# Gathers over more tiles, ELU's operations after the third block sum, ScalarE's block copies first at step 5

## The chip, the cores and the metric

The kernel runs on one core of a Trainium2 chip. The metric is the time of one execution on the device in microseconds, the median of several runs. A profiled execution gives the times of single instructions.

## The reference, cut to what matters

2048 samples, 10 time steps, tables for region and point of interest, a convolution over three steps with ELU, then two LSTM layers of 256 units over 8 steps, and three linear layers with no nonlinearity between them.

```
rp = concatenate([region_tbl[region_idx], poi_tbl[poi_idx]], -1)
nv = concatenate([rp @ W_rp + b_rp, coords @ W_co + b_co], -1)
conv = elu(conv1d(nv, conv_w) + conv_b)
emb = tanh(concatenate([car_tbl[car_idx], week_tbl[week_idx], time_tbl[time_idx]], -1))
x = concatenate([conv, broadcast(emb)], -1)
h = lstm_layer(x, Wih0, Whh0, bih0, bhh0)
h = lstm_layer(h, Wih1, Whh1, bih1, bhh1)
return ((h[:, -1] @ W1 + b1) @ W2 + b2) @ W3 + b3
# lstm step: i, f, g, o = split(x @ Wih.T + h @ Whh.T + bias)
#            c = sigmoid(f) * c + sigmoid(i) * tanh(g);  h = sigmoid(o) * tanh(c)
```

## The kernel before

The samples are worked on in four batches of 512 columns, numbered 0 to 3 (in `stages`, `n`). Every engine runs its own list of instructions, written out by hand; all of them walk through the same list of stages, and semaphores tie them together. There is no scheduler: the order in the code is the order on the engine.

A **cell** is one step of one layer. Layer 0's cell of step t ("lower") and layer 1's cell of step t-1 ("upper") alternate. A cell has eight tiles: two halves j of the state for each of the four gates, 128 x 512 each. After a tile TensorE raises `gate_acc[0]` or `gate_acc[1]`, which VectorE, ScalarE and the gathers wait for. All products are of fp16 high and low parts, three for each fp32 product.

In steps 1 to 5 of batches 1 to 3 (steps 4 and 5 in batch 0) the upper cell is a **fast** one (`fast_cell` in TensorE's part): fourteen block products of 128 x 256 in the manner of Strassen, twelve matmuls each, and not 192 matmuls of 512 columns. It uses PSUM banks A1, A2 (in `aux`) and B1, B2, E1, E2 (in `acc`). The first two products fill A1 and A2. ScalarE copies A1 to B1 and A2 to B2 (`upper_acts`, L1006); the third product adds to B1 and so waits for the first copy, the fourth for the second. Later ScalarE copies E1, A1, E2 and A2 into `gates1` (L1013 to L1022). VectorE adds the second form to them in `part_sums` (L1622), four sums in a cell; the twelfth product reuses A1 and waits for the second of these sums.

VectorE's part of the stages is `lower` (eight `add_embeddings`, L1379, one for each tile of the lower cell, between the operations of the upper cell before it) and `upper`. In both, `both_ig`, `both_fc`, `both_c`, `both_h` and `both_lo` are the LSTM's elementwise operations over 128 x 1024, and `t_forms`, `t_low` make sums of h's blocks for the next fast cell.

Three things for the following batch lie between these:

- **ELU** of the second half of the features (`elu_piece`, nine pieces numbered 0 to 8, 1 to 4 being a reciprocal over 128 columns each, 5 and 6 a product and a sum, 7 and 8 the high and low part of the result). VectorE does pieces 0 to 3 in the lower cell of step 2 and the others in `upper` of step 1 (`low.makes_x`), in batches 1 to 3. SyncE then loads the result into `x_in`; step 4 is the first to use it.
- **The turn**: before step 5's upper cell TensorE transposes the gathered features and embeddings of the next batch (`turn`, c = 0, and `turn_emb`). ScalarE copies the features out of PSUM (`put_turned`) and takes two tanh of the embeddings (`emb_tanhs`); VectorE makes the low part (`split_emb`). That is in batches 0 to 2. The second half of the features is turned in the next batch, after its first upper cell.
- **Gathers** (GpSimd, `pool` in the code, POOL in the rows): per batch 8 of the embeddings and 48 of region and point of interest for the first six time steps, then 32 for the last four. Each is an indirect DMA of 128 rows. `pace` names cells as (layer, step); before a gather POOL waits until the tile that the generator `tiles` gives it has been made. Step 8 and 9 mean steps 0 and 1 of the next batch.

Of the kernel before, what the change touches and what calls it, by code (L numbers as in the profile page):

```python
# [47 lines left out]
ADDS7 = 4  # L48
# [11 lines left out]
class Cell:  # L60
# [3 lines left out]
    def __init__(self, layer, t, counts, bank0, before, slots=None, first=False, last=False, batch=None,  # L64
# [8 lines left out]
        self.forms_of = None  # L73
        self.opens7 = False
        self.early = False
        self.makes_x = False
# [78 lines left out]
def stages(eng, nbatch, steps):  # L155
# [10 lines left out]
    def body(n, following, opened=None):  # L166
# [50 lines left out]
        if following:  # L217
            yield "turn", n + 1, 0
            yield "turn_emb", n + 1
        end = fast(last_t - 2)  # L220
        yield "upper", end, low[1]
        low = lower(last_t, end)
# [37 lines left out]
def build(nc, d):  # L260
# [20 lines left out]
    GR = NCOL // P  # L281
# [14 lines left out]
    with ExitStack() as ctx:  # L296
# [365 lines left out]
        def _(pool):  # L662
# [66 lines left out]
            for n in range(NB):  # L729
# [64 lines left out]
                else:  # L794
# [7 lines left out]
                    if n == 1:  # L802
                        pool.wait_ge(idx_ready, 3)
                    begun = list(pace(n, [(0, 3), (1, 2), (0, 4), (1, 3), (0, 5), (1, 4)]))
                    rows = GR * (2 + 2 * WIN)
# [4 lines left out]
                    copy_emb()  # L810
                    tiles = pace(n, [(1, 5), (0, 7), (1, 6), (0, 8)])
                    gather_steps(WIN, T, True, rows_in[1])

        @block.scalar
        def _(act):
# [185 lines left out]
            def upper_acts(s, low):  # L1001
                steps, sums = s.fast * STEPS7, s.fast * ADDS7
                act.wait_ge(h_done[1], ahead + s.half)
                for bank, source, step in ((B1, A1, 1), (B2, A2, 2)):
                    act.wait_ge(part_acc, steps + step)
                    nc.scalar.copy(bank, source).then_inc(part_copy, 1)  # L1006
                for bank, pair, step in ((B1, (GATE_I, GATE_G), 3), (B2, (GATE_F, GATE_O), 4)):
                    act.wait_ge(part_acc, steps + step)
                    for a, g in enumerate(pair):
                        quarter(s, 0, g, LEFT, half_bank(bank, a))  # L1010
                tanh_both(low)
                act.wait_ge(part_acc, steps + 5)
# [86 lines left out]
            for stage in stages(act, NB, STEPS):  # L1099
                kind = stage[0]  # L1100
                if kind == "turn":
                    n, c = stage[1:]
                    put_turned(feat_t[:, c, :], aux[0:KF, c, :], turned[c], n + 1, turned_put[c])
                elif kind == "turn_emb":
                    emb_tanhs(stage[1], aux[:, 2, :])
                elif kind == "emb_gates":
                    put_emb_gates(*stage[1:])
                elif kind == "conv":
                    elu_parts(chunk_of(*stage[1:]), slice(0, NCOL))
                elif kind == "lower":  # L1110
                    lower_acts(*stage[1:])
                elif kind == "upper":
                    upper_acts(*stage[1:])
                elif kind == "rest":
                    tanh_both(stage[1])
                    put_h_hi(stage[1])
                elif kind == "cell":
                    final_acts(stage[1]) if stage[1].final else cell_acts(stage[1])

        @block.vector  # L1120
        def _(dve):
# [463 lines left out]
            def lower(s, tail, plain_tail):  # L1585
# [17 lines left out]
                else:  # L1603
# [6 lines left out]
                    for k, place in enumerate(places[4:]):  # L1610
                        add_embeddings(s, *place)
                        if s.makes_x:
                            elu_piece(chunk_of(s.batch, 1), s.batch, k)
# [10 lines left out]
            def upper(s, low):  # L1624
# [3 lines left out]

                x_piece(4)
                both_ig(low)  # L1630
                both_fc(low)
                both_c(low)
                x_piece(5)
                x_piece(6)
                both_h(low)
                if low.forms is not None:
                    t_forms(low)
                both_lo(low)
                x_piece(7)
                part_sums(s, 0)  # L1640
                if low.forms is not None:
                    t_low(low)
                x_piece(8)
                for k in range(1, ADDS7):
                    part_sums(s, k)
                both_ig(s)

# [98 lines left out]
            for stage in stages(dve, NB, STEPS):  # L1746
                kind = stage[0]
                if kind == "turn_emb":
                    split_emb(stage[1])
                elif kind == "conv":  # L1750
                    n, c = stage[1:]
# [559 lines left out]
```

## Time and profile before

| what | us |
|---|---|
| median of 3 runs | 1069.15 (1068.37 to 2749.66) |
| the profiled execution | 1068.24 |
| its span, first to last instruction | 1066.4 |
| TensorE busy in it | 1027.5 |
| VectorE, ScalarE, GpSimd busy | 810.0, 668.1, 351.0 |

The median is that of the runs shown, the longest of which is disturbed. In the rows, PE is TensorE (PEld its weight loads), DVE VectorE, ACT ScalarE, POOL GpSimd. Batch 1's steps lie from about 337 us, batch 2's from 587, batch 3's from 836; one batch takes some 249 us.

### The profile page before, as it was taken

How to read it: one execution, taken by the hardware profiler on the slowest of the kernel's cores; microseconds unless marked ns; L12 is line 12 of the kernel's file. 1: busy time of each engine (PE TensorE's matmuls, PEld its weight loads, DVE VectorE, ACT ScalarE, POOL GpSimd, SP SyncE). 2: the span in 40 equal slices, each digit the busy share in tenths (PEclk: the TensorE clock that was granted, in tenths of full speed). 3: DMA queues.
4: the chain of work that ended last, by engine and by line, in shares of the span. 5: the costliest groups of instructions: out<-in, count | busy, mean ns of one | idle time of the engine just before them, and what ended most of it. 6: DMA issues, size and time to landing. Idle time of an engine off the chain costs nothing.

```text
span 1066.4 us, 15685 instructions
## 1 busy us (share of the span) xinstructions
PE 1027.5 (96%) x6129; PEld 627.9 (59%) x6129; DVE 810.0 (76%) x1135; ACT 668.1 (63%) x1029; POOL 351.0 (33%) x353
## 2 busy tenths in 40 slices
PE   8699999999999999999999999999999999999997
PEld 6444444477445666676545567766644577666645
DVE  5489889976768878677787886777686887878654
ACT  2466444577565767777664676767755577777743
POOL 7660066645430046553540025663631000000000
PEclk9799999999999999999999999999999999999999
DMA  9310100000111010000010110000010100000001
GB/s 258 80 18 14 30 3 2 3 2 2 14 21 40 2 33 2 3 2 2 2 32 1 40 32 3 3 3 2 3 31 2 40 22 10 1 1 2 1 1 40
DMA packets 32092, 21.43 MB, mean 20 GB/s; under 512 B 19629, under 2 KB 25865, under 8 KB 32019
## 3 DMA queue, kind: packets, MB, share of 16 engines
q1 hardware_dynamic: 21223, 19.25, 6.3%
q0 software_dynamic: 9984, 1.12, 2.7%
q8 instruction: 48, 0.79, 0.3%
q14 instruction: 25, 0.20, 0.1%
q10 hardware_dynamic: 812, 0.07, 0.1%
HBM read 9.92 MB, written 4.19 MB: 13 GB/s over the span
## 4 chain that ended last, share of the span: by engine, by line
PE 80%; DVE 11%; issue 4%; ACT 4%; another core or an unknown queue 0%; DVEq 0%; POOL 0%; ACTq 0%; POOLq 0%
PE acc L1967 29%; PE acc L2001 13%; PE aux L2001 13%; PE acc L1958 12%; PE acc L1952 4%; DVE gates L1379 2%; PE aux L2282 2%; PE acc L1779 2%; ACT gates L938 1%; DVE h_part L1581 1%; DVE t_part L1546 1%; DVE h_full L1574 1%; PE acc L2107 1%; PE acc L2116 1%; PE aux L1867 1%
## 5 line engine op out<-in xcount | busy, mean ns | idle before, releaser
L1967 PE MATMUL acc<-h_part,wh 128*128 128x512 f16 x1824 | 445.9, 380 | 0.0
L1967 PEld LDWEIGHTS acc<-h_part,wh 128*128 128x128 f16 x1824 | 160.4, 98 | 217.6 <-issue 53.5
L740 POOL DMA_INDIRECT feat<-in_L_rec_region_tbl,region_idx x160 | 173.6, 1085 | 148.8 <-PE aux L2001 45.8
L1379 DVE TENSOR_TENSOR gates<-acc,emb_gates 128x512 f32<-128x512 f32 x239 | 157.1, 682 | 22.8 <-PE acc L1967 16.1
L938 ACT ACTIVATE gates<-gates,gate_bias,unscale 128x512 f32<-128x512 f32 x168 | 128.3, 806 | 65.0 <-DVE gates L1379 62.8
L740 POOL DMA_INDIRECT feat<-in_L_rec_poi_tbl,poi_idx x120 | 132.4, 1103 | 93.5 <-PE acc L1967 33.9
L1958 PE MATMUL acc<-h_part,wh 128*128 128x512 f16 x624 | 148.6, 379 | 0.3
L1952 PE MATMUL acc<-x_in,wx 96*128 96x512 f32 x239 | 132.8, 562 | 0.8 <-DVE gates L1379 0.8
L923 ACT ACTIVATE gates<-acc,gate_bias,unscale 128x512 f32<-128x512 f32 x110 | 81.8, 780 | 77.1 <-PE acc L1967 54.0
L1958 PEld LDWEIGHTS acc<-h_part,wh 128*128 128x128 f16 x624 | 59.8, 98 | 75.5 <-issue 4.4
L2001 PE MATMUL aux<-t_part,w_form 128*128 128x256 f16 x816 | 94.8, 273 | 0.0
L966 ACT ACTIVATE gates<-gates,gate_bias,unscale 128x256 f32<-128x256 f32 x136 | 75.2, 593 | 25.1 <-DVE gates L1622 23.7
L1574 DVE TENSOR_TENSOR h_full<-gates 128x1024 f32<-128x1024 f32 x38 | 46.6, 1227 | 53.9 <-ACT gates L945 50.0
L2001 PEld LDWEIGHTS aux<-t_part,w_form 128*128 128x128 f16 x816 | 79.8, 98 | 9.5 <-ACT gates L1022 0.3
L923 ACT ACTIVATE gates<-gates,gate_bias,unscale 128x512 f32<-128x512 f32 x74 | 57.3, 810 | 33.8 <-DVE gates L1379 29.9
L2001 PE MATMUL acc<-h_part,wh 128*128 128x256 f16 x408 | 49.4, 278 | 13.3 <-ACT acc L1006 9.5
L1952 PEld LDWEIGHTS acc<-x_in,wx 96*128 96x128 f32 x239 | 45.2, 190 | 27.7 <-issue 2.2
L1581 DVE TENSOR_TENSOR h_part<-h_full,h_part 128x1024 f16<-128x1024 f32 x38 | 46.4, 1222 | 15.2 <-ACT h_part L951 15.2
L932 ACT ACTIVATE gates<-cell_c 128x512 f32<-128x512 f32 x50 | 31.4, 627 | 40.9 <-DVE cell_c L1408 24.0
L945 ACT ACTIVATE gates<-cell_c 128x1024 f32<-128x1024 f32 x38 | 40.1, 1056 | 21.0 <-DVE cell_c L1567 20.0
L2001 PEld LDWEIGHTS acc<-h_part,wh 128*128 128x128 f16 x408 | 38.9, 99 | 23.8 <-ACT acc L1006 13.8
L2001 PE MATMUL aux<-t_part,wh 128*128 128x256 f16 x408 | 50.1, 273 | 2.8 <-DVE gates L1622 2.8
(239 smaller groups left out, 1451.7 us busy)
## 6 DMA issues: line engine op xcount, KB each, us to landing
out<-y SPq DMA_DIRECT2D x16, 256.0 KB, 2.1
x_in<-conv_hi SPq DMA_DIRECT2D x56, 64.0 KB
feat<-in_L_rec_region_tbl,region_idx POOLq DMA_INDIRECT x160
w<-in_L_rec_W SPq DMA_DIRECT2D x4, 512.0 KB, 5.2
w_nat<-in_L_rec_Whh SPq DMA_DIRECT2D x2, 1024.0 KB, 8.3
w<-in_L_rec_W SPq DMA_DIRECT2D x1, 2048.0 KB
feat<-in_L_rec_poi_tbl,poi_idx POOLq DMA_INDIRECT x120
x_in<-conv_lo SPq DMA_DIRECT2D x28, 64.0 KB
```

Of the source, the lines that this page charges most:

```text
L740: pool.indirect_dma_start(out, None, tables[k], bass.IndirectOffsetOnAxis(ap=rows, axis=0)).then_inc(landed, DMA)
L923: nc.scalar.activation(gates[layer][:, j, g, :], source, ACT.Tanh if g == GATE_G else ACT.Sigmoid, bias=gate_bias[:, layer, m:m + 1], scal ...
L938: nc.scalar.activation(gates[0][:, j, g, :], gates[0][:, j, g, :], ACT.Tanh if g == GATE_G else ACT.Sigmoid, bias=gate_bias[:, 0, m:m + 1] ...
L945: nc.scalar.activation(gates[layer][:, :, GATE_I, :], cell_c[layer][:, :, :], ACT.Tanh).then_inc(tanh_c_done[layer], HK)
L966: op = nc.scalar.activation(gates[1][:, j, g, cols], source, ACT.Tanh if g == GATE_G else ACT.Sigmoid, bias=gate_bias[:, 1, m:m + 1], scal ...
L1379: nc.vector.tensor_tensor(gates[0][:, j, g, :], source, emb_gates[:, g * HK + j, :], ALU.add).then_inc(gate_sum, 1)
L1574: nc.vector.tensor_tensor(h_full[:, :, :], gates_of(s, GATE_O), gates_of(s, GATE_I), ALU.mult).then_inc(h_full_done[layer], HK)
L1581: nc.vector.tensor_tensor(h_part[layer][:, s.write_slot, LO, :, :], h_full[:, :, :], h_part[layer][:, s.write_slot, HI, :, :], ALU.subtrac ...
L1952: mm = nc.tensor.matmul(bank, wx[:, rows], x_in[:, s.t, :], start=True, stop=s.first)
L1958: mm = nc.tensor.matmul(bank, wh[:, 1, a, c, rows], h_part[0][:, s.write_slot, b, c, :], start=(c == 0 and a == b == HI), stop=(s.first an ...
L1967: mm = nc.tensor.matmul(bank, wh[:, own_w, a, c, rows], h_part[layer][:, s.read_slot, b, c, :], start=False, stop=(c == HK - 1 and a == LO))
L2001: mm = nc.tensor.matmul(bank[:, cols], weights(left, layer, w, g), moving(right, layer, x), start=(opens and a == layer == 0 and w == x == ...
```

## The change

Three edits, and no matmul moves.

First, the gathers' generator. The first set of 56 was spread over the 48 tiles of (0,3), (1,2), (0,4), (1,3), (0,5), (1,4); now over 60, from (1,1) to the fourth tile of (0,6). The second set of 32 took one tile after the other of (1,5), (0,7), (1,6), (0,8), 30 tiles; now it is spread over 44, to the sixth tile of (0,9).

Second, on VectorE ELU's pieces 5 and 6 stand after the third block sum and not before `both_h`, piece 7 after the fourth sum, piece 8 after `both_ig`, piece 4 after `both_c`.

Third, at step 5's upper cell ScalarE makes the copies A1 to B1 and A2 to B2 first, then the feature copy, four gate activations, and then the two tanh of the embeddings. VectorE's `split_emb` stands behind `both_c`. The cell knows by `feeds` for which batch.

```diff
         end = fast(last_t - 2)
+        end.feeds = n + 1 if following else None
         yield "upper", end, low[1]
...
-                    begun = list(pace(n, [(0, 3), (1, 2), (0, 4), (1, 3), (0, 5), (1, 4)]))
+                    begun = list(pace(n, [(1, 1), (0, 3), (1, 2), (0, 4), (1, 3), (0, 5), (1, 4), (0, 6)]))[:-4]
                     rows = GR * (2 + 2 * WIN)
                     tiles = (begun[i * len(begun) // rows] for i in range(rows))
...
-                    tiles = pace(n, [(1, 5), (0, 7), (1, 6), (0, 8)])
+                    begun = list(pace(n, [(1, 5), (0, 7), (1, 6), (0, 8), (1, 7), (0, 9)]))[:-2]
+                    rows = GR * 2 * (T - WIN)
+                    tiles = (begun[i * len(begun) // rows] for i in range(rows))
...
                     act.wait_ge(part_acc, steps + step)
                     nc.scalar.copy(bank, source).then_inc(part_copy, 1)
+                if s.feeds is not None:
+                    put_turned(feat_t[:, 0, :], aux[0:KF, 0, :], turned[0], s.feeds + 1, turned_put[0])
                 for bank, pair, step in ((B1, (GATE_I, GATE_G), 3), (B2, (GATE_F, GATE_O), 4)):
...
+                if s.feeds is not None:
+                    emb_tanhs(s.feeds, aux[:, 2, :])
                 tanh_both(low)
...
-                        if s.makes_x:
+                        if s.makes_x and k < 3:
                             elu_piece(chunk_of(s.batch, 1), s.batch, k)
...
-                x_piece(4)
+                x_piece(3)
                 both_ig(low)
                 both_fc(low)
                 both_c(low)
-                x_piece(5)
-                x_piece(6)
+                if s.feeds is not None:
+                    split_emb(s.feeds)
+                x_piece(4)
...
-                x_piece(7)
                 part_sums(s, 0)
                 if low.forms is not None:
                     t_low(low)
+                part_sums(s, 1)
+                part_sums(s, 2)
+                x_piece(5)
+                x_piece(6)
+                part_sums(s, 3)
+                x_piece(7)
+                both_ig(s)
                 x_piece(8)
-                for k in range(1, ADDS7):
-                    part_sums(s, k)
-                both_ig(s)
```

How the order on the engines changes, at the two places that the prediction speaks of. On ScalarE, step 5's upper cell, before: the `feat_t` row is the feature copy, `emb_tanh` and `emb_in` the two tanh, `acc<-aux` the copies of A1 and A2.

```order
L938 ACTIVATE gates<-gates,gate_bias,unscale 128x512 x5
L879 COPY feat_t<-aux 84x512
L900 ACTIVATE emb_tanh<-aux 128x512
L901 ACTIVATE emb_in<-aux 128x512
L1006 COPY acc<-aux 128x512 x2
L966 ACTIVATE gates<-acc,gate_bias,unscale 128x256 x4
L945 ACTIVATE gates<-cell_c 128x2x512
L1013 COPY gates<-acc 128x2x256
```

And after:

```order
L942 ACTIVATE gates<-gates,gate_bias,unscale 128x512 x5
L1010 COPY acc<-aux 128x512 x2
L883 COPY feat_t<-aux 84x512
L970 ACTIVATE gates<-acc,gate_bias,unscale 128x256 x4
L904 ACTIVATE emb_tanh<-aux 128x512
L905 ACTIVATE emb_in<-aux 128x512
L949 ACTIVATE gates<-cell_c 128x2x512
L1021 COPY gates<-acc 128x2x256
```

The two block copies went to the front, and the two tanh now stand directly before the cell state's tanh (`gates<-cell_c`).

On VectorE, step 1's upper cell, from `both_h` on, before. `elu_part`, `conv_hi` and `conv_lo` are ELU's pieces 5 to 8, `gates<-acc,gates` and `gates<-aux,gates` the block sums.

```order
L1352 SCALAR_TENSOR_TENSOR elu_part<-elu_part 128x512
L1357 TENSOR_TENSOR elu_part<-elu_part 128x512
L1574 TENSOR_TENSOR h_full<-gates 128x1024
L1533 TENSOR_TENSOR t_full<-h_full 128x512
L1536 TENSOR_TENSOR t_full<-h_full,t_full 128x256
L1539 TENSOR_TENSOR t_full<-h_full,t_full 128x256
L1581 TENSOR_TENSOR h_part<-h_full,h_part 128x1024
L1361 CAST conv_hi<-elu_part 128x512
L1622 TENSOR_TENSOR gates<-acc,gates 128x2x256
L1546 TENSOR_TENSOR t_part<-t_full,t_part 128x1024
L1364 TENSOR_TENSOR conv_lo<-elu_part,conv_hi 128x512
L1622 TENSOR_TENSOR gates<-aux,gates 128x2x256 x2
```

And after:

```order
L1588 TENSOR_TENSOR h_part<-h_full,h_part 128x1024
L1629 TENSOR_TENSOR gates<-acc,gates 128x2x256
L1553 TENSOR_TENSOR t_part<-t_full,t_part 128x1024
L1629 TENSOR_TENSOR gates<-aux,gates 128x2x256 x2
L1359 SCALAR_TENSOR_TENSOR elu_part<-elu_part 128x512
L1364 TENSOR_TENSOR elu_part<-elu_part 128x512
L1629 TENSOR_TENSOR gates<-acc,gates 128x2x256
L1368 CAST conv_hi<-elu_part 128x512
L1561 TENSOR_TENSOR ig<-gates 128x1024
L1371 TENSOR_TENSOR conv_lo<-elu_part,conv_hi 128x512
L1567 TENSOR_TENSOR cell_c<-gates,cell_c 128x1024
```

The last four pieces went behind the second and third sum, two of them behind the fourth sum too. POOL's list keeps its order; only the tile that each gather waits for is another.

## Rows read from the trace of the kernel before

**Rows 1.** The page: busy times (us, share, instructions), and the chain that ended last.

```profile
PE 1027.5 (96%) x6129; PEld 627.9 (59%) x6129; DVE 810.0 (76%) x1135; ACT 668.1 (63%) x1029; POOL 351.0 (33%) x353
...
PE 80%; DVE 11%; issue 4%; ACT 4%; another core or an unknown queue 0%; DVEq 0%; POOL 0%; ACTq 0%; POOLq 0%
```

**Rows 2.** Windows: steps 2 to 4 of batches 1, 2, 3; length, then busy times.

```profile
391.00:490.20 99.20, 93.41 (x674) 65.44 (x673) 73.58 (x92) 70.53 (x108) 54.57 (x52) 1.00 0.04 3
640.50:739.50 99.00, 94.34 (x674) 66.35 (x673) 73.92 (x92) 70.57 (x108) 55.08 (x51) 0.98 0.05 3
889.80:982.50 92.70, 92.55 (x673) 65.78 (x672) 73.59 (x92) 70.64 (x108) 0.00 (x0) 1.00 0.00 1
```

The columns are window, length, busy time and count of PE, PEld, DVE, ACT and POOL, then the granted clock of TensorE, DMA share and GB/s.

**Rows 3.** Windows, TensorE alone: single cells. Length, busy, granted clock, DMA share, GB/s.

```profile
411.40:423.80 12.40, 12.40 (x59) 1.00 0.04 2
423.80:444.70 20.90, 18.65 (x170) 1.00 0.04 3
...
491.00:510.10 19.10, 18.48 (x171) 1.00 0.03 2
640.50:662.90 22.40, 19.84 (x169) 0.92 0.05 4
...
675.30:694.10 18.80, 18.66 (x170) 1.00 0.05 3
...
889.80:908.30 18.50, 18.45 (x169) 1.00 0.00 1
```

The first is a lower cell, the others are fast upper cells.

**Rows 4.** Timeline of batch 1, start of step 3's upper cell: start, length, instruction, idle before.

```profile
423.85 2.78 PE L2001 MATMUL aux<-h_part,wh 128*128 128x256 f16 x24
...
424.58 0.95 POOL L740 DMA_INDIRECT feat<-in_L_rec_poi_tbl,poi_idx  x1 [0.30 <-issue]
...
425.83 1.25 POOL L740 DMA_INDIRECT feat<-in_L_rec_region_tbl,region_idx  x1 [0.30 <-issue]
...
428.26 0.57 ACT L1006 COPY acc<-aux 128x512 f32<-128x512 f32 x1 [2.06 <-remote]
428.88 2.29 PE L2001 MATMUL acc<-h_part,wh 128*128 128x256 f16 x18 [2.25 <-issue]
...
430.03 0.94 POOL L740 DMA_INDIRECT feat<-in_L_rec_region_tbl,region_idx  x1 [1.70 <-PE acc L2001]
```

**Rows 5.** Timeline of batch 1, step 1's upper cell; last row batch 3's lower cell.

```profile
362.00 2.79 PE L2001 MATMUL acc<-h_part,wh 128*128 128x256 f16 x24 [0.77 <-ACT acc L1006]
...
371.19 0.42 DVE L1361 CAST conv_hi<-elu_part 128x512 fp32r<-128x512 f32 x1
...
373.38 0.68 DVE L1364 TENSOR_TENSOR conv_lo<-elu_part,conv_hi 128x512 fp32r<-128x512 f32 x1
373.98 1.28 DVE L1622 TENSOR_TENSOR gates<-aux,gates 128x512 f32<-128x512 f32 x2
...
374.72 1.48 PE L2001 MATMUL aux<-t_part,wh 128*128 128x256 f16 x12 [0.76 <-DVE gates L1622]
...
377.55 0.69 DVE L1622 TENSOR_TENSOR gates<-acc,gates 128x512 f32<-128x512 f32 x1 [2.29 <-PE acc L2001]
...
882.34 0.69 DVE L1379 TENSOR_TENSOR gates<-acc,emb_gates 128x512 f32<-128x512 f32 x1 [0.40 <-PE acc L1967]
```

**Rows 6.** Timeline of batch 1, the turn and step 5's upper cell.

```profile
492.14 0.97 POOL L740 DMA_INDIRECT feat<-in_L_rec_region_tbl,region_idx  x1 [11.58 <-PE aux L2001]
492.37 0.56 ACT L879 COPY feat_t<-aux 84x512 f32<-84x512 f32 x1
...
493.80 1.06 ACT L1006 COPY acc<-aux 128x512 f32<-128x512 f32 x2
494.01 1.40 DVE L1372 TENSOR_TENSOR emb_in<-emb_tanh,emb_in 32x512 fp32r<-32x512 f32 x2 [2.61 <-ACT emb_in L901]
494.44 2.79 PE L2001 MATMUL acc<-h_part,wh 128*128 128x256 f16 x24 [0.62 <-ACT acc L1006]
```

**Rows 7.** Waits over the whole span: us in total, times, longest us.

```profile
POOL feat L740 <- DMA feat<-in_L_rec_region_tbl,region_idx: 8.5, 5, 2.4
```

More of the change, by code:

```diff
@@ L74, in __init__ @@
         self.opens7 = False
+        self.feeds = None
         self.early = False
@@ L1102, in _ @@
                     n, c = stage[1:]
-                    put_turned(feat_t[:, c, :], aux[0:KF, c, :], turned[c], n + 1, turned_put[c])
-                elif kind == "turn_emb":
-                    emb_tanhs(stage[1], aux[:, 2, :])
+                    if c == 1:
+                        put_turned(feat_t[:, 1, :], aux[0:KF, 1, :], turned[1], n + 1, turned_put[1])
                 elif kind == "emb_gates":
@@ L1747, in _ @@
                 kind = stage[0]
-                if kind == "turn_emb":
-                    split_emb(stage[1])
-                elif kind == "conv":
+                if kind == "conv":
                     n, c = stage[1:]
```

## The prediction

> **What bounds the kernel now.** Read the page first: TensorE is busy 1027.5 of 1066.4 us, and the chain that ended last is 80% its own [rows 1]. So the kernel is bound by TensorE, and a change that touches no matmul can only give back TensorE's idle time, 38.9 us in all, a good part of it in the opening and at the last head, which the change leaves alone. Two per cent, which is about what a measurement of this kernel can tell from no change, would be 21.4 us.
>
> Next the same work in different batches. From the start of step 2's upper cell to the turn before step 5's (three upper and three lower cells), batches 1, 2 and 3 run the same 670-odd matmuls. They take 99.20, 99.00 and 92.70 us [rows 2]. The columns show one difference: POOL is busy 54.6 and 55.1 us in the first two and 0 in the third, because batch 3 gathers for nobody. VectorE and ScalarE do the same work in the same time (73.6 and 70.6 us). So the gathers cost 6.5 + 6.3 = 12.8 us, though no engine works a microsecond longer for them. This is the largest term that anything here can move.
>
> Where it is lost: in the fast upper cells. One takes 18.5 us without gathers, but 20.90 and 22.40 us with them, and a third only 18.80 [rows 3]. The lower cells do not differ. The 22.40 us cell holds a second effect, a mean granted clock of 0.92, that is some 3.5 us at the lower level of 1.2 GHz, right after the longest wait of TensorE in the steps.
>
> What the loss looks like from near: at 423.85 TensorE issues its first two products, 24 matmuls, done by 426.6. ScalarE's copy of the first one starts only at 428.26, 2.06 us idle, though its product had been finished for over 2 us; the next product waits for that copy [rows 4]. Beside it POOL issues gather after gather with 0.30 us between them, and after the stall it is back to waiting for TensorE (1.70 us idle). So a signal from TensorE arrives late while POOL runs without a pause. I found this same pattern (ScalarE or VectorE starting 0.5 to 2.9 us after the product it waits for) at a dozen places of batches 1 and 2, each beside such an unpaused run, and at none of the fast cells of batch 3.
>
> **Gathers over more tiles.** Why does POOL run unpaused? The first set has 56 gathers over 48 tiles, 1.17 for each tile. A lower tile takes 1.54 us (its 8 tiles fill 12.4 us), so a gather is allowed each 1.32 us. One takes 0.95 to 1.25 us and 0.30 between [rows 4], 1.25 to 1.55 us. POOL falls behind in every lower cell and carries the backlog into the next upper cell, whose first copies are the tightest place of the program. After the change 56 gathers lie on 60 tiles: 0.93 a tile, one each 1.65 us in lower cells and each 2.8 us in upper ones. I replayed the waits with the tile times of this trace and 1.4 us a gather: in batches 1 and 2 the longest run of late gathers falls from 12 to 1 or 2. In batch 0 it grows, since the indices are ready only at 131 us when all eight tiles of (1,1) are over: about 20 gathers run unpaused to 160 us. There the cells are plain ones; unpaused runs of 7 and more lie beside them in this trace and no TensorE wait follows, so I take 0 for it.
>
> Bounds of this term: 0 if the cost goes by gathers and not by backlog, 12.8 if all goes. The nearest row for paced gathers is step 5's upper cell, beside which the second set runs at one a tile: 19.10 us [rows 3], 18.5 and the 0.6 us stall of the copies treated below; so paced gathers cost it nothing. The gathers now also lie beside step 1's upper cell in batches 1 and 2; for those two I leave 0.3 each, as the 18.80 us cell lost. Term: 12.8 - 0.6 = **12.2 us**.
>
> The second set (32 gathers over 44 tiles and not 30) moves only in the cells around the batch border, where I found no TensorE wait over 0.1 us. 0, and its last gather, at tile 5 of the next batch's step 1, is some 17 us ahead of the turn that needs it.
>
> A rule speaks against spreading as the cure. Rows first: VectorE's 92 instructions take 73.58, 73.92 and 73.59 us with and without gathers [rows 2]; they do not lose to POOL. The Trainium skill ("SBUF — State Buffer", "Who interferes with whom") holds that only the port pair shared by VectorE and GpSimd causes contention, an exclusive lock. By it the price would go with each gather, wherever it stands, which is the first rival below. The trace does not agree: the late signals run from TensorE to ScalarE.
>
> **ELU's parts.** In step 1's upper cell (batches 1 to 3) VectorE has to sum a block product before TensorE may issue the twelfth. TensorE waits 0.76 us for it at 374.72, since the cast at 371.19 (0.42) and the subtraction at 373.38 (0.68) stand before the sums at 373.98 [rows 5]. The change puts both behind, along with the two operations of 0.68 each: the second and third sums come about 1.1 us earlier and the 0.76 goes. What is late next: the idle 2.29 us before the fourth sum (377.55) holds the two 0.68 pieces for free, but the cast and the subtraction now stand between the fourth sum and the forget-gate product, 1.1 us on a VectorE that is nearly full through the following lower cell. Its slack there is 0.40 at the third embedding sum [rows 5] and little elsewhere. About 0.5 us therefore comes back at the first copies of step 2's upper cell, whose wait is 0.05 us in batch 3. Net 0.76 - 0.5 = 0.26, three times: **0.8 us**, bounds 0 and 2.3. The 0.77 us wait at 362.00 stays: the ScalarE activations ahead of it follow embedding sums that are not moved. The reciprocal that moves behind the cell state's sum fills a gap while ScalarE makes the tanh: 0. ELU's result is ready some 5 us later, and its twelve loads of x then end near 390 us, 20 us before step 4 needs them: 0.
>
> **ScalarE's copies first.** At step 5 TensorE waits 0.62 us at 494.44, because the feature copy and two tanh (492.37 to 493.91) stand before the copies of the block products, which start at 493.80 when ScalarE was free at 492.45 [rows 6]. With the copies first the wait goes. The feature copy then runs before the third product is done, free. The two tanh, 1.07 us, now stand before the tanh of the cell state and so before the third copy; and VectorE's two 0.7 us splits (494.01) move behind the cell state's sum, where they wait for those tanh and hold h_full back. I estimate the third copy just at the product that needs it, 0.2 us late. Net 0.4, in batches 0 to 2: **1.2 us**, bounds 0 and 1.9.
>
> **Sum.** 12.2 + 0.8 + 1.2 = 14.2 us. Against the profiled execution, 1068.24 us, that is 1054.0. It lies 0.9 us under the median of the runs shown (1069.15), which gives **1055.0 us**.
>
> **Rivals.**
> First, the cost goes by the gather: 12.8 us over 112 gathers is 0.11 us each, whatever the pace. Then only ELU and the copies remain, 2.0 us: 1067.1. For it: in batch 2 one cell lost only 0.3 us beside a run as dense. Against it: step 5's upper cell, paced, loses nothing. The Trainium skill's port rule above would end here.
> Second, half of the late signals stay, since they come wherever two gathers follow closely, and pairs remain at each upper cell's end where one product counts for two tiles: 6.1 + 2.0 gives 1061.
> Third, slower: the cost goes by each fast cell that has gathers beside it. There were six (12.8 us, 2.1 each); there will be eight, because the first set now also covers step 1's upper cell, where two waits already show that copies and sums are just in time. 17.0 - 12.8 = 4.2 more, less 2.0: 1071.3. It decides if a paced fast cell still loses more than 1.85 us. Against it again step 5's upper cell.
> Fourth, the turn waits: the last gather of the first set moves from 477.6 to about 483, beside the lower cell of step 6. POOL had 11.58 us idle there [rows 6], the turn stands at 490.17, and the longest wait of POOL for a landing is 2.4 us [rows 7], so some 4 us are left. Were POOL 5 us late the turn would lose 1 us a batch: 1058.
>
> **How the numbers follow.** Forecast 0.62; half stays 0.20; by the gather 0.08; slower by the cell 0.05; the turn waits 0.05. Low end: all bounds at their best, 12.8 + 2.3 + 1.9 = 17, 1052.2, and a little under it for runs that differ by 0.7 us. High end: a third of the gather term, 1064.5, which takes in the second and fourth rival; only the two others lie outside. Range 1051.5 to 1064.5. Faster by over 2% would need more than all idle time that the change touches: 0.01. Slower by over 2% is further than any rival: 0.01. Within 2%: 0.98.
>
> **What the profile after would show.** The stretches of rows 2 at 93 us in all batches; no unpaused run of gathers longer than two in batches 1 and 2, and POOL waiting for TensorE between them; clock 1.00 throughout. In step 1's upper cell no TensorE wait for the sums, but a wait of some 0.5 us for the first copies one step later. In step 5's no wait at the first copies, perhaps 0.2 us at the third. The forecast fails if late signals appear beside single gathers, or if the 20 unpaused gathers of batch 0 now stall TensorE between 131 and 160 us.

## The result, and the profile after

The changed kernel takes 1060.24 us (median of 20 runs, 1053.33 to 1062.26); the kernel before took 1065.89 beside it (20 runs, undisturbed ones from 1058.82 to 1069.35). The ratio is 0.995, 95% interval 0.9934 to 0.9966: 5.7 us less by the medians, where 14.2 were forecast. The forecast time of 1055.0 is 5.2 us short. The profiled execution took 1059.06, its span is 1057.3.

The stretches of [rows 2], now (columns as there):

```profile
396.20:489.50 93.30, 92.56 (x674) 65.85 (x673) 74.19 (x92) 70.54 (x108) 49.62 (x44) 1.00 0.04 3
638.10:731.40 93.30, 92.56 (x673) 65.78 (x672) 74.19 (x92) 70.55 (x108) 50.32 (x44) 1.00 0.04 3
880.00:973.30 93.30, 92.55 (x674) 65.79 (x672) 74.18 (x93) 70.55 (x108) 0.00 (x0) 1.00 0.00 1
```

All three are equal, with gathers and without. The fast upper cells of steps 3, 4 and 5 in batch 1 now take this (TensorE alone, columns as in [rows 3]), all at a clock of 1.00. Before, steps 3 and 5 took 20.90 and 19.10 us:

```profile
427.70:446.40 18.70, 18.65 (x170) 1.00 0.04 3
458.60:477.30 18.70, 18.65 (x170) 1.00 0.04 2
490.40:509.10 18.70, 18.70 (x172) 1.00 0.03 2
```

The place of [rows 4], start of step 3's upper cell in batch 1, in the timeline after:

```profile
427.71 2.78 PE L2010 MATMUL aux<-h_part,wh 128*128 128x256 f16 x24
...
429.52 1.37 POOL L742 DMA_INDIRECT feat<-in_L_rec_region_tbl,region_idx  x1 [0.30 <-issue]
429.91 1.19 ACT L1010 COPY acc<-aux 128x512 f32<-128x512 f32 x2
...
430.54 2.79 PE L2010 MATMUL acc<-h_part,wh 128*128 128x256 f16 x24
...
431.64 1.74 POOL L742 DMA_INDIRECT feat<-in_L_rec_poi_tbl,poi_idx  x1 [0.75 <-PE acc L2010]
```

ScalarE's copy no longer shows an idle time, and TensorE goes on 0.05 us after its first 24 matmuls. At the place of [rows 5], the sums of step 1's upper cell and the lower cell after it:

```profile
379.94 1.47 PE L2010 MATMUL aux<-t_part,wh 128*128 128x256 f16 x12
380.14 0.69 DVE L1629 TENSOR_TENSOR gates<-aux,gates 128x512 f32<-128x512 f32 x1 [0.62 <-issue]
380.75 0.68 DVE L1359 SCALAR_TENSOR_TENSOR elu_part<-elu_part 128x512 f32<-128x512 f32 x1
...
382.81 0.69 DVE L1629 TENSOR_TENSOR gates<-acc,gates 128x512 f32<-128x512 f32 x1 [0.66 <-PE acc L2010]
383.42 0.42 DVE L1368 CAST conv_hi<-elu_part 128x512 fp32r<-128x512 f32 x1
...
399.01 1.05 ACT L1010 COPY acc<-aux 128x512 f32<-128x512 f32 x2
399.64 2.79 PE L2010 MATMUL acc<-h_part,wh 128*128 128x256 f16 x24 [0.64 <-ACT acc L1010]
```

The 0.76 us wait for the sums is gone, and 0.64 us comes back at the first copies of step 2, since the cast and the subtraction stand behind the fourth sum. And at the place of [rows 6]:

```profile
490.36 2.78 PE L2010 MATMUL aux<-h_part,wh 128*128 128x256 f16 x24
...
491.92 0.57 ACT L1010 COPY acc<-aux 128x512 f32<-128x512 f32 x1
...
492.98 2.78 PE L2010 MATMUL acc<-h_part,wh 128*128 128x256 f16 x24
...
493.66 0.58 ACT L883 COPY feat_t<-aux 84x512 f32<-84x512 f32 x1
```

No wait is left there. So batches 1 to 3 did what was forecast. Batch 0 did not. Its timeline, around the plain cells of steps 2 and 3:

```profile
144.44 0.69 DVE L1386 TENSOR_TENSOR gates<-acc,emb_gates 128x512 f32<-128x512 f32 x1 [3.59 <-remote]
...
146.86 0.95 POOL L742 DMA_INDIRECT feat<-in_L_rec_poi_tbl,poi_idx  x1 [0.30 <-issue]
...
148.63 0.38 PE L1967 MATMUL acc<-h_part,wh 128*128 128x512 f16 x1 [1.00 <-issue]
...
150.07 0.69 DVE L1386 TENSOR_TENSOR gates<-acc,emb_gates 128x512 f32<-128x512 f32 x1 [4.34 <-remote]
...
150.30 0.95 POOL L742 DMA_INDIRECT feat<-in_L_rec_region_tbl,region_idx  x1 [2.50 <-remote]
...
174.71 0.49 PE L1961 MATMUL acc<-x_in,wx 96*128 96x512 f32 x1 [3.89 <-DVE gates L1386]
```

From 130.25 GpSimd issues 14 gathers with 0.30 us between them, since the indices are ready only then and the tiles of (1,1) are long made. Beside the last of them VectorE starts late twice in a row, after 3.6 and 4.3 us of idle time, on tiles of the lower cell that TensorE had finished by 141.4. It is not VectorE alone: GpSimd's own 15th gather comes after 2.50 us that the profile puts down to nothing it knows ("remote"), and TensorE, which has banks in hand and waits for no engine in the middle of a tile, issues four matmuls of one tile at intervals of 0.7 to 1.4 us where 0.22 is usual. So more is slow here than one engine's signals. VectorE falls behind by this; at 174.71 TensorE waits 3.89 us for it and then runs at 1.2 GHz for 3.5 us (granted clock 0.51), which costs 1.7 more.

What it cost in all is read by comparing the same matmuls in both traces. The changed kernel's execution was 1.4 us ahead of the one before from 72 to 146 us, by an opening that no edit touches; at 150 it is 1.2 us behind, from 175 on 7.0. So this burst of gathers cost 8.4 us: 2.6 at the four slow issues and 5.8 at the long wait and behind it. Step 4's upper cell starts at 216.67 and not, as before, at 209.73.

The two profiled executions (spans 1066.4 and 1057.3) so differ by -9.1 us, which the starts of the cells split: -1.4 in the opening; +8.4 in batch 0 up to step 4; -11.6 from step 2's to step 5's upper cell of batches 1 and 2, a sum in which +1.2 of the new step 2 wait is held, so -12.8 by the gathers; -2.7 in the three step 1 cells and +1.8 back behind them, net -0.9 by ELU; -2.4 behind the three step 5 cells, by the copies.

Below, a signal is called late where an engine starts long after the work it waits for and the trace names nothing else. The rows show the late start; that a signal was on its way so long is a reading of it.

### The profile page after: what moved, and what is told of

The parts are those of the page before. It is cut to its first block and busy times, and to the rows that moved or that the text cites. A ratio compares the mean times of both kernels' runs of the same rounds, so it can differ in the third digit from the quotient of the medians.

```text
span 1057.3 us, 15682 instructions
## 1 busy us (share of the span) xinstructions
PE 1024.7 (97%) x6129; PEld 627.5 (59%) x6129; DVE 809.7 (77%) x1135; ACT 666.6 (63%) x1029; POOL 352.5 (33%) x353
## 3 DMA queue, kind: packets, MB, share of 16 engines
q0 software_dynamic: 9984, 1.12, 2.8%
## 5 line engine op out<-in xcount | busy, mean ns | idle before, releaser
L1976 PEld LDWEIGHTS acc<-h_part,wh 128*128 128x128 f16 x1824 | 160.8, 98 | 218.7 <-issue 55.6
L1967 PEld LDWEIGHTS acc<-h_part,wh 128*128 128x128 f16 x624 | 59.8, 98 | 77.7 <-issue 7.4
L955 ACT CAST h_part<-h_full 128x1024 f16<-128x1024 f32 x38 | 39.7, 1046 | 16.5 <-DVE h_full L1581 16.4
L2010 PE MATMUL acc<-h_part,w_form 128*128 128x256 f16 x408 | 50.1, 273 | 0.0
```

The lines of the kernel that those rows point to most:

```text
L1967: mm = nc.tensor.matmul(bank, wh[:, 1, a, c, rows], h_part[0][:, s.write_slot, b, c, :], start=(c == 0 and a == b == HI), stop=(s.first an ...
L1976: mm = nc.tensor.matmul(bank, wh[:, own_w, a, c, rows], h_part[layer][:, s.read_slot, b, c, :], start=False, stop=(c == HK - 1 and a == LO))
L2010: mm = nc.tensor.matmul(bank[:, cols], weights(left, layer, w, g), moving(right, layer, x), start=(opens and a == layer == 0 and w == x == ...
```

## The experiments

Eighteen runs, of nine kernels, were made in five sessions; in each, the kernel before ran on the same chip beside them. The sessions fall into two kinds, which decided more than I had thought. In the first session (e1 to e4) the kernel before took 1068.5 us and in the last (h1, h2) 1066.9, as in the result above. In the three others it took 1046.9, 1046.9 and 1046.7, and all its runs but one (1158.98) lie within 2.5 us of that. I call the first kind late sessions and the second prompt ones, by the signals. Times are compared within a session only.

**e1_b0_start**: pace batch 0's first set from the tiles that come once the indices are ready.

```diff
-                    begun = list(pace(n, [(1, 1), (0, 3), (1, 2), ...]))[:-4]
+                    own = [(0, 3), (1, 2), (0, 4), (1, 3), (0, 5), (1, 4), (0, 6)]
+                    begun = list(pace(n, own if n == 1 else [(1, 1)] + own))[:-4]
```

> The changed kernel with one edit: in batch 0 the first set of gathers is spread over the tiles from (0,3) on, not from (1,1), so that 56 gathers lie on 52 tiles and none is allowed long before the indices are ready. Theory (late signals come from gathers that run without a pause, and 16 of them in batch 0 cost the changed kernel 7 us between 140 and 217 us): step 4's upper cell of batch 0 starts near 209.5 us again and not at 216.7, no TensorE wait of more than 1 us between 130 and 209, span 7 us under the 1057.3 of the changed kernel. Rival (batch 0's loss comes from ELU's or ScalarE's edits, or from chance): the start stays at 216 or moves by chance, span within 2 us of 1057.

Measured (late session): 1053.14 us (1051.8 to 1054.17), ratio 0.9857 (0.9832 to 0.9882), span 1050.0. Step 4's upper cell starts at 209.1. The long run is gone (the longest is now of seven, 132 to 140 us), and so is the whole loss of batch 0. All of TensorE's waits from 75 to 1030 us, as us in total, times, longest: first the changed kernel's, then e1's.

```profile
PE acc L1961 <- DVE gates L1386: 4.6, 2, 3.9
PE acc L2010 <- ACT acc L1010: 4.2, 6, 0.8
PE acc L1967 <- issue: 1.9, 4, 1.0
```

```profile
PE acc L2011 <- ACT acc L1011: 4.2, 6, 0.8
PE acc L1962 <- DVE gates L1387: 0.7, 1, 0.7
```

What e1 keeps are the six known waits of 0.77 and 0.64 us and one of 0.7, which the kernel before has too (0.8). It beats both kernels, and the one before by 15.4 us, more than was forecast of the change.

**e2_pace_only**: the kernel before with the new pacing of both sets, ELU and the copies as before.

> The kernel before with the new pacing of both sets alone. Theory: steps 2 to 4 of batches 1 and 2 take 92.7 us each, as batch 3's, and not 99; batch 0 loses 7 us; the waits of 0.76 us for the block sums and 0.62 us for ScalarE's copies stay. Net 12.8 - 7 = 5.8 us faster than the kernel before. Rival (the cost goes by the gather): 99 us stay.

Measured: 1063.89 us, ratio 0.9958 (0.9934 to 0.9981), span 1064.1. Its batches 1 and 2:

```profile
401.00:493.70 92.70, 92.55 (x674) 65.83 (x673) 73.61 (x91) 70.61 (x108) 50.09 (x44) 1.00 0.04 3
644.20:737.00 92.80, 92.62 (x674) 65.85 (x673) 73.68 (x91) 70.60 (x108) 50.77 (x44) 1.00 0.04 3
```

Pacing alone takes away all of the 12.8 us: 92.7 is what batch 3 takes without gathers [rows 2]. And pacing alone makes batch 0 lose: step 4's upper cell starts at 219.6, and 9.4 us of that are lost between 146 and 182 us against the same matmuls of the kernel before. The wait in it:

```profile
176.62 0.79 PE L1954 MATMUL acc<-x_in,wx 96*128 96x512 f32 x1 [4.14 <-DVE gates L1381]
```

**e3_rest_only**: the changed kernel with the old pacing of both sets.

> The changed kernel with the old pacing of both sets, so the edits of ELU and ScalarE alone. Theory: steps 2 to 4 of batches 1 and 2 take 99 us as in the kernel before, give or take 2, batch 0 has its step 4 at 210; the wait for the sums in step 1 is gone, 0.64 us stand at step 2's first copies, step 5's wait is gone. Net 0.3 us for each of three ELU and 0.6 for each of three turns: 2 to 3 us faster than the kernel before, inside the noise. Rival (the two edits cured the late signals): 93 us in batches 1 and 2 and 13 us or more faster.

Measured: 1067.41 us, ratio 0.9977 (0.995 to 1.0004), span 1067.2. The late signals are back where gathers run unpaused:

```profile
397.82 1.06 ACT L1008 COPY acc<-aux 128x512 f32<-128x512 f32 x2 [2.58 <-remote]
397.93 0.94 POOL L742 DMA_INDIRECT feat<-in_L_rec_region_tbl,region_idx  x1 [1.80 <-remote]
398.44 1.03 PEld L2008 LDWEIGHTS acc<-h_part,wh 128*128 128x128 f16 x7 [3.64 <-ACT acc L1008]
398.44 1.29 PE L2008 MATMUL acc<-h_part,wh 128*128 128x256 f16 x6 [3.36 <-ACT acc L1008]
```

The two small edits alone are worth little that can be measured in a late session, 0 to 5 us by the interval. The profiled execution is even 0.8 us longer than that of the kernel before. From step 2's to step 5's upper cell, batches 1 and 2 take 103.0 and 99.1 us in it (100.0 and 99.8 in the kernel before); the first is more than expected. It loses 2.9 us in batch 0 as well, just ahead of step 4. Against the same instructions of the kernel before VectorE starts two tiles 0.5 and 0.7 us later, at 174.09 and 176.29, beside five gathers 0.30 us apart (167.67 to 173.6); some 28 us later TensorE waits 2.02 us for it and then runs 3.4 us at a granted clock of 0.50. The kernel before has the same pacing there and lost nothing. So plain cells can lose beside short runs too, and not in every execution.

How often an engine idled for a reason that the profile does not know ("remote") from 75 to 1030 us bears this out: 9 times in the kernel before (12.2 us in all, ScalarE 4, VectorE 1, GpSimd 4), 8 times in e3, 3 times in the changed kernel, all at the burst in batch 0, and never in e1, nor in g1 and h2 below.

**e4_memsets**: as the changed kernel, but the gathers for batches 1 to 3 are left out; at the same places and the same pace stands a short zero fill of the same tile.

> The changed kernel with each gather of batches 1 to 3's inputs replaced by a fill of the same columns with zeros on GpSimd, at the same pace; it leaves the gathers out and shows what is left without any gather DMA. Theory: batch 0 no longer loses, step 4's upper cell starts at 209 us or earlier; batches 1 and 2 as in the changed kernel, 92.9 us. Span 1050. If batches 1 and 2 get faster than that, the paced gathers still cost something.

Measured: 1052.77 us, ratio 0.9847 (0.981 to 0.9885), span 1049.8. GpSimd has little to do then (4.8 us busy in batch 1's steps 2 to 4, where it was 49.5 with e1's gathers). The span is 0.2 us under e1's 1050.0 and the same stretch takes 92.9 us against e1's 93.0, so paced gathers cost next to nothing. That excludes a cost by the gather (the first rival) and one by the fast cell (the third).

**e5_all_before_fourth**: e1, and ELU's pieces 5 to 8 all between the third and the fourth block sum.

```diff
                 x_piece(5)
                 x_piece(6)
-                part_sums(s, 3)
                 x_piece(7)
-                both_ig(s)
                 x_piece(8)
+                part_sums(s, 3)
+                both_ig(s)
```

> The kernel with batch 0's pacing from (0,3), and ELU's last four pieces all between the third and the fourth block sum. Theory of the ELU term: TensorE's wait of 0.64 us at the first copies of step 2's upper cell, three times, comes from the cast and the subtraction that stand behind the fourth sum and push VectorE's chain through the lower cell; the fourth sum has 1.9 to 2.3 us of idle time before it, the four pieces take 2.4, so the chain is pushed by 0.5 and the 0.4 of slack takes that up. Expected: that wait falls to 0.1 us, 1.6 us less in all against the kernel with batch 0's pacing alone (span 1050.0), so 1048.4. Rival (the wait belongs to the seam between the cells whatever VectorE does): 0.64 stays.

Measured (prompt session): 1041.61 us, ratio 0.995 (0.9936 to 0.9963). As expected, the wait at step 2's first copies is nearly gone, 0.14 us, and the stretches of batches 1 to 3 are 92.80 us and not 93.30. What a late session would give was not measured.

**e6_unpaced**: the changed kernel with the first set unpaused (56 gathers in a row in each batch), the second at the old pace.

```diff
-                    begun = list(pace(n, [(1, 1), (0, 3), (1, 2), ...]))[:-4]
-                    tiles = (begun[i * len(begun) // rows] for i in range(rows))
+                    begun = list(pace(n, [(0, 3)]))
+                    tiles = iter(begun[:1])
```

> The changed kernel with the first set of gathers without pace: all 56 run as soon as the first tile of (0,3) is made; the second set has its old pace. Theory (a run without a pause makes signals late): the run lasts some 75 us in each of batches 0, 1, 2; each fast cell beside it loses 2 us or more, and the plain cells of batch 0 lose 7 us or more; span 1075 or more. Rival (backlog at the seam to an upper cell is what costs, not the run): 1 or 2 us a batch.

Measured: 1043.96 us, ratio 0.9974 (0.9964 to 0.9983). This is a clear miss of my theory as I had put it: by it every batch would lose. But the kernel before was 20 us faster too. In that session no signal is late beside whatever run of gathers.

**e7_spacer**: the changed kernel with a fill of 0.55 us on GpSimd ahead of each gather of batch 0's sets.

> The changed kernel, in which POOL in batch 0's first set fills 512 columns of a scratch tile before each gather, some 0.6 us, with the waits for tiles unchanged. The gathers are as late as in the changed kernel, but 1.9 us apart and not 1.25. Theory (dense issue of gathers makes signals late): batch 0 loses little, step 4's upper cell starts at 209 to 211 us. Rival (POOL's being behind, or gathers beside these very cells, costs): 216 as in the changed kernel.

Measured: 1042.95 us, ratio 0.9965 (0.9952 to 0.9978). There was no loss in batch 0 for it to cure.

**e8_busy_no_dma**: as e6, but with a fill of 128 x 768 in place of each gather; all gathers but the first batch's own are left out.

```diff
+                    if n:
+                        spaced[0] += 1
+                        pool.wait_ge(zeroed, spaced[0])
+                        nc.gpsimd.memset(spacer[:, :], 0.0).then_inc(zeroed, 1)
+                    else:
                         pool.indirect_dma_start(out, None, tables[k], ...)
```

> As the one without pace, but in batches 1 to 3's inputs each gather is a fill of 768 columns of a scratch tile, some 0.8 us, so it leaves the gathers out: POOL is as busy without a pause, and sends no DMA. If the DMAs that POOL issues are what makes signals late, nothing is lost and the span is some 1050. If POOL's instructions and their semaphore increments without a pause are enough, it loses as the one without pace does.

Measured: 1044.35 us, ratio 0.9977 (0.9968 to 0.9986), no different from e6, and no news for the same reason.

**f1 to f4** are the kernels of e6, e7, e8 and e5 again, in the hope of a late session.

> The kernel without pace for the first set once more, since its first run was on a chip on which the kernel before takes 1046.9 us and no signal was late at all. If this run is on a chip on which the kernel before takes over 1060: the theory that dense gathers make signals late there expects 1075 or more, since all 56 of a set run without a pause. The rival (only backlog at the seam between cells costs) expects 1 or 2 us a batch against the kernel before.

> The kernel with fills between batch 0's gathers once more, for the same reason. On a chip with late signals the theory expects step 4's upper cell of batch 0 at 209 to 211 us (216.7 in the changed kernel there) and a span within 2 us of 1050; the rival expects 1057.

> The kernel with fills in place of the gathers once more; it leaves the gathers of batches 1 to 3 out. On a chip with late signals: 1050 if the gathers' DMAs are the cause, 1075 as the one without pace if POOL's instructions alone are.

> The best version once more: batch 0's pacing from (0,3), ELU's last four pieces before the fourth sum. On the first chip of this kind it took 1041.6 against 1046.9 before. On a chip with late signals it should be at 1051.5, 1.6 us under the one with batch 0's pacing alone (1053.14) and 15 us under the kernel before.

Measured, again a prompt session: 1043.81, 1043.58, 1044.33, 1041.41 us; ratios 0.9973, 0.9969, 0.998, 0.9948, each within 0.0005 of the session before.

**g1 to g4**, the same four once more:

> The changed kernel with the first set of gathers unpaused from the first tile of step 1's lower cell on (56 in a row in every batch), the second set at the old pace. Theory (unpaused gathers delay signals, on chips that show late signals): 6 us and more are lost in each of batches 0, 1 and 2, a ratio of 1.00 to 1.01 and a span 15 us or more over that of g2. If this chip is like the two of the calls before (kernel before at 1047 us and no late signals), the ratio is 0.997 again and the run tells nothing new.

> The changed kernel with a fill of 0.55 us on GpSimd ahead of each gather of batch 0's two sets, so that the gathers there follow each other at 1.9 us and not 1.3. If it is the density of the DMAs, batch 0 loses nothing and the ratio is near 0.986 on a chip with late signals. If it is that GpSimd never pauses, batch 0 loses 7 us as in the changed kernel, 0.993 to 0.995.

> As g1, but in the batches after the first a fill on GpSimd of 0.8 us stands in place of each gather: GpSimd as busy, no indirect DMA (the features and embeddings of batches 1 to 3 are left out). If the gathers' DMAs delay the signals, batches 1 and 2 lose nothing, span 12 us or more under g1. If GpSimd's unpaused instructions do, the span is that of g1.

> The changed kernel with batch 0's first set paced from the second tile of step 1's lower cell and all four ELU pieces between the third and the fourth block sum. On a chip with late signals both gains should add: 7 us of batch 0 and 1.5 us of the copies at step 2, a ratio of 0.984 to 0.986. On a calm chip 0.995 as before.

Two of these name the wrong cell: in g1 and g4 the pacing begins with step 3's lower cell, as in e6 and e1.

Measured, prompt a third time: 1043.53, 1042.61, 1043.96, 1041.2 us; ratios 0.997, 0.9965, 0.9975, 0.9952. In g1's windows, with real gathers unpaused, the stretch of batch 0 in which the changed kernel lost, and batch 1's steps 2 to 4:

```profile
129.10:172.10 43.00, 43.00 (x200) 19.45 (x199) 38.12 (x62) 20.25 (x28) 32.94 (x34) 1.00 0.07 3
380.40:473.80 93.40, 92.52 (x673) 65.81 (x672) 74.31 (x93) 70.50 (x108) 54.20 (x51) 1.00 0.05 3
```

TensorE does not idle once in the first, and the second is 0.1 us over a paced one.

**h1_after_again** and **h2_busy_no_dma**: the changed kernel unedited, and the kernel of e8.

> The changed kernel itself, unedited. On a chip without late signals (kernel before near 1047 us) only the two small terms are left, 0.76 and 0.6 us three times with 0.6 us coming back each time: some 3 us, a ratio of 0.997, and batch 0 loses nothing. On a chip with late signals 0.993 to 0.997, with batch 0's loss of 7 us.

> Unpaused gathers in batch 0 and, in the batches after it, unpaused fills of 0.8 us in place of the gathers (the features and embeddings of batches 1 to 3 are left out). On a chip with late signals: if the gathers' DMAs delay them, batch 0 alone shows them; if GpSimd's unpaused instructions do, batches 1 and 2 show them too, 6 us each. On a chip without them, a ratio of 0.9975 again.

This was a late session (before: 1066.87 us). h1: 1056.44 us (1055.16 to 1061.28), ratio 0.9913 (0.9883 to 0.9942), a little better than expected. Its profiled execution, at 1058.8 one of the longer of the five, loses 9.5 us in batch 0, at the same instructions as the changed kernel did; what the shorter ones lost is not on record. h2: 1053.31 (1052.53 to 1054.01), ratio 0.9882 (0.9858 to 0.9906). The expectation of h2 has a slip: the gathers that lie in batch 0 are those for batch 1, so h2 has fills there too, and unpaused gathers only in the opening. So the two are compared at the same place, 138 to 181 us of batch 0. h1's window first, h2's second:

```profile
138.00:181.00 43.00, 37.21 (x156) 15.88 (x153) 30.53 (x50) 15.17 (x21) 21.75 (x21) 0.92 0.05 3
```

```profile
138.00:181.00 43.00, 43.00 (x199) 19.44 (x198) 39.32 (x62) 20.49 (x28) 37.95 (x50) 1.00 0.00 1
```

GpSimd is far busier with the fills (37.95 us against 21.75), and TensorE loses nothing; with the gathers it idles 5.8 us and its granted clock is 0.92. h2's batch 1, with fills unpaused, is no slower than with paced gathers:

```profile
389.30:482.60 93.30, 92.55 (x674) 65.83 (x673) 74.53 (x93) 70.53 (x108) 33.14 (x45) 1.00 0.01 1
```

So fills back to back on GpSimd delay no signal. It takes the gathers' indirect DMAs, and a late session. The kernel of e6, with the first set's gathers unpaused, never ran in one, so h2 lacks its exact counterpart.

## Why the prediction was wrong

**The step that failed** is the sentence on batch 0: "There the cells are plain ones; unpaused runs of 7 and more lie beside them in this trace and no TensorE wait follows, so I take 0 for it." In its place the runs show a loss of 8.4 us in the profiled execution, 9.4 in e2 and 9.5 in h1, and none in e1, where the burst is gone. The replay had shown a run of 20 (14 came close together), and the last line of the prediction names it as what would break it. What misled me is that I looked for a wait of TensorE beside the run. In a plain cell TensorE has banks in hand, so a late signal first shows as idle time of VectorE, and as the long wait of TensorE only 25 us later. And runs of 7 are no row for a run this long: e1 has one of seven and loses nothing, while e3 loses 2.9 us beside one of five. I gave the sum one value for an effect that I had just named as the cause of the largest loss. One to three such signals at the 2.1 us that a fast cell lost would have given a bound of 2 to 6 us, still under the 8.4.

**Gathers in batches 1 and 2**: right. 12.2 were forecast, 12.8 measured; e2 shows that pacing alone does it, e4 that paced gathers cost next to nothing, e3 that without it the late signals stay.

**ELU**: net 0.8 forecast, 0.9 measured. The two parts were each a little larger, 0.91 and 0.60 in place of 0.76 and 0.5. "Little slack elsewhere" held; the better place is e5's.

**ScalarE's copies**: 1.2 forecast, 2.4 in the profiled execution, 0.81 a batch. The third copy, for which I had taken 0.2 us off, shows no wait. The rest is in how I read the rows. Where nothing waits, the third product starts 0.16 us before the end that the row gives for the first 24 matmuls (490.36 + 2.78 = 493.14, but 492.98). A wait counted from that end is short by as much: the 0.62 cost 0.78, and ELU's 0.76 cost 0.92.

**The rivals**: the first ends with e4. Of the second ("half stays") the number was near, 1061, by luck and not by its mechanism: nothing of the signals stayed in batches 1 and 2, and no pair of gathers stalled anything. For the same reason it is luck that the time lies in the stated range, which was made wide for the gathers' term and not for batch 0. Its upper end is no clean sum either: a third of that term alone gives 1065.1, with the two small ones 1063.1. The third ends with e4, the fourth with the turn at 489.5, which shows no wait.

**The base**: the profiled execution of before (1068.24) and the median of 3 (1069.15) lie 2 to 3 us above the median of 20, 1065.89. In terms: from 1068.24, forecast 14.2; measured 9.2, that is 16.1 by the three terms and 1.4 by the opening, less 8.4. From the medians it is 5.7, because the execution with the trace was among the longer ones of before and 1.2 us under the median of the changed kernel.

**What the size depends on**: in the prompt sessions, where no signal is late, what pacing can give is next to nothing (1043.96 us unpaced in e6, 1042.95 paced in e7). There only the two small edits are left, 3.3 to 4.1 us (e7, f2, g2: 0.9965 to 0.9969). The changed kernel unedited had no run in a prompt session. In the two late sessions it gained 5.7 and 10.4 us; its own runs there reach from 1053 to 1062 us, where e1's six, which have no such burst, lie within 2.4 us.

**Open** is why sessions differ. The last session ran on the chip of the same number as the first prompt one, so the number alone doesn't tell them apart. One rival that no run tested is the recorder: every timed execution here has its span and clock on record, so none shows the kernel without it, and the traces differ in what they kept. For the same 9984 packets on the gathers' queue they hold 4451 to 5283 records of semaphore updates by DMAs in the late sessions and 7391 to 7426 in the prompt ones. Whether recording takes part in the lateness is not known. Open too is whether in a late session a pause between gathers of 0.6 us is enough (the spacer never met one), how many gathers in a row it takes, which part of an indirect DMA delays the signals, whether it is signals or the issue of instructions that is slow (TensorE's four matmuls look like the second), and what e5 gives there: an estimate from e1 and its 0.5 us in each of three batches is 0.984, which no run has shown.

## What to carry to other kernels

Where a consumer starts long after its product and the trace names no reason, look at which DMAs are issued beside it, and spread them over the work with a wait on progress for each. When such a wait is put on progress, check the first time that it is reached: what has long been passed paces nothing, and the backlog runs off in one burst. And look for the damage not only at the bound engine: in a stage with buffers in hand it shows first as idle time of the engines behind it. A kernel tuned by such effects should be timed in more than one session, since here one kernel (e1) was worth 15 us in one of them and its nearest kin (e7, f2, g2) 3 to 4 us in others.

## What the runs showed of the hardware

**Signals can be late, or not, as the session is.** The kernel before differs by 20 us between sessions. 12.8 us are those of [rows 2]. The kernel before has no trace from a prompt session, but e1 (late) and e5 (prompt) pace their gathers alike: e5 is 8.9 us ahead at 80 us and 7.0 at step 4's upper cell (202.1 against 209.1). So most of the rest lies in the opening, where gathers run unpaused in every version. These are windows of the first 80 us, of the changed kernel's late execution and of g1's prompt one:

```profile
0.00:80.00 80.00, 64.37 (x285) 41.06 (x286) 50.33 (x105) 36.94 (x77) 53.90 (x78) 0.91 0.48 120
```

```profile
0.00:80.00 80.00, 70.55 (x337) 45.50 (x338) 58.84 (x120) 44.32 (x89) 52.30 (x77) 0.98 0.50 124
```

The DMAs move about the same, 120 and 124 GB/s, and GpSimd is as busy. But TensorE has issued 285 matmuls in the one and 337 in the other. The timeline of the changed kernel has this there:

```profile
42.24 0.59 ACT L867 CAST wh<-aux 128x512 f16<-128x512 f32 x1 [2.92 <-remote]
...
43.61 1.11 PE L1801 MATMUL aux<-ident,w_nat 128*128 128x128 f32 x4 [6.91 <-DVE wh L1220]
```

ScalarE and VectorE start late after TensorE's products, as in the cells, and in the wait of 6.9 us TensorE's clock falls as well: from 38.8 to 49.1 it was granted 0.50 (the mean of the 80 us is 0.91, against 0.98). That the opening's late signals have the same cause was not tested: no run paced it.

**A late signal costs more than itself through the clock.** In e2 the wait of 4.14 us leaves TensorE at 1.2 GHz from 175.2 to 182.1:

```profile
175.20:182.10 6.90, 5.48 (x13) 0.51 0.01 2
```

At a granted 0.51 some 2.7 us of work are lost in the 5.5 us that TensorE is busy of these 6.9 (an estimate from this row), two thirds of the wait once more. The Trainium skill ("SBUF — State Buffer", "Who interferes with whom") knows an exclusive lock of VectorE and GpSimd as the way in which engines disturb each other; this case does not fit it. VectorE's busy time is the same with and without gathers (73.58 and 73.59 us [rows 2]), and the late starts are ScalarE's and GpSimd's too, and TensorE's issue. h2 alone would not settle it, since a fill is not a gather.
